# Value projection of a diffusion attention: two blocks a batch in place of four, one for two groups of heads

## The reference, cut to what matters

```
h = layernorm(x) * ln1_w + ln1_b
qk = (h @ Wqk).reshape(b, n, 16, 16).transpose(0, 2, 1, 3)
v = (h @ Wv).reshape(b, n, 16, 16).transpose(0, 2, 1, 3)
logits = (2 * qk @ qk^T - |qk_n|^2 - |qk_m|^2) / 4 * tau
out = softmax(logits) @ v        # per head, 512 x 512
y = out @ Wo
```

## Time and profile before

| | |
|---|---|
| time, median of 3 | 4381.61 us |
| the profiled execution | 4382.84 us, its span 4381.0 us |
| PE busy, whole span | 3709.8 us (85%) |
| DVE, ACT, POOL busy | 2415.1, 1752.6, 1619.3 us |
| the stage of the change | about 2767 to 3790 us of the span, with its head start and its end |
| granted TensorE clock over the span | 0.924 |
| value blocks (L2276) | 32 blocks, 512 PE instructions |

### The profile page before, as it was taken

One profiled execution on the slowest core, in us unless ns is written; L12 is line 12 of the kernel. 1 busy time (PEld: TensorE's weight loads), 2 busy tenths in 40 slices (PEclk: granted clock), 3 DMA queues, 4 the chain that ended last, 5 costly groups with the idle time before them and its releaser, 6 DMA issues. The chain is left out here.

```text
span 4381.0 us, 64166 instructions
## 1 busy us (share of the span) xinstructions
PE 3709.8 (85%) x17520; PEld 2209.8 (50%) x17584; DVE 2415.1 (55%) x6529; ACT 1752.6 (40%) x4010; POOL 1619.3 (37%) x1750
## 2 busy tenths in 40 slices
PE   6999999999689998997999899679999998459940
PEld 3555555566345555554555555335555554346630
DVE  6766676677465662224656433245566665345556
ACT  2544444455345554112555511035555545114420
POOL 2333333333466762004667512401222221352244
PEclk8999999999799999999999999879999999669975
DMA  6555665557201112443011211132222221249952
GB/s 103 71 74 68 84 84 79 71 65 92 67 25 39 48 43 99 158 164 105 34 38 48 74 46 60 41 79 53 61 56 54 54 50 47 89 166 312 312 169 70
DMA packets 230366, 378.28 MB, mean 86 GB/s; under 512 B 39822, under 2 KB 166099, under 8 KB 223699
## 3 DMA queue, kind: packets, MB, share of 16 engines
q1 hardware_dynamic: 216658, 355.13, 34.4%
q0 software_dynamic: 6144, 16.79, 1.2%
q10 hardware_dynamic: 7296, 3.22, 0.3%
HBM read 170.03 MB, written 84.93 MB: 58 GB/s over the span
## 5 line engine op out<-in xcount | busy, mean ns | idle before, releaser
L758 DVE CUSTOM_DVE_ANT_0 a_ps<-a_ps,a_mask 128x128 f32<-128x128 f32 (+3 forms) x1024 | 481.0, 513 | 219.1 <-PE a_ps L513 199.6
L2618 DVE TENSOR_REDUCE c_neg_max<-c_ps 128x1 f32<-128x512 f32 x512 | 340.8, 684 | 244.5 <-PE c_ps L2286 243.1
L2479 ACT ACTIVATE c_probsT<-c_ps 128x512 f32<-128x512 f32 x512 | 299.2, 598 | 400.1 <-PE c_ps L2298 391.2
L368 POOL TENSOR_SCALAR_AFFINE_SELECT a_probs_c<-a_probs_c 128x256 f32<-128x256 f32 (+1 forms) x384 | 185.8, 500 | 699.5 <-ACT a_probs_c L663 699.2
L663 ACT ACTIVATE a_probs_c<-a_ps 128x512 f32<-128x512 f32 x640 | 344.6, 603 | 119.5 <-PE a_ps L531 84.4
L513 PE MATMUL a_ps<-a_packed_qk 65*128 65x128 f32 (+3 forms) x1024 | 336.9, 373 | 53.5 <-DVE a_maxima L758 28.0
L1094 POOL TENSOR_TENSOR w_probs<-w_probs,w_inv 128x1024 f32<-128x1024 f32 x128 | 242.3, 1893 | 334.8 <-DVE w_inv L1457 334.8
L549 PE MATMUL a_ps<-a_probs_c,a_v 128*64 128x512 f32 (+3 forms) x2048 | 329.9, 468 | 1.8 <-POOL a_probs_c L368 0.8
L531 PE MATMUL a_ps<-a_packed_qk 67*128 67x512 f32 (+3 forms) x1024 | 288.8, 345 | 0.8 <-DMA a_packed_qk<-a_max_half 0.8
L2286 PE MATMUL c_ps<-c_packed_qk 68*128 68x512 f32 x512 | 263.2, 519 | 4.4 <-DVE c_neg_max L2618 2.2
L1349 ACT ACTIVATE w_probs<-w_ps_s,w_neg_max 128x256 f32<-128x256 f32 x512 | 236.0, 478 | 68.2 <-DVE w_neg_max L1452 66.9
(11 more groups left out here) (323 smaller groups left out, 7805.9 us busy)
## 6 DMA issues: line engine op xcount, KB each, us to landing
a_packed_qk<-a_halves SPq DMA_DIRECT2D x512, 128.0 KB, 4.6
d_w<-in_L_ffn_second SPq DMA_DIRECT2D x71, 516.0 KB, 5.0
d_w<-in_L_ffn_first SPq DMA_DIRECT2D x71, 512.0 KB, 5.1
rows_dram<-f_zeros SPq DMA_DIRECT2D x8, 4096.0 KB, 16.1
c_packed_qk<-c_halves SPq DMA_DIRECT2D x256, 128.0 KB, 2.4
w_v<-w_v_next SPq DMA_DIRECT2D x16, 1024.0 KB, 4.7
d_rows<-rows_dram SPq DMA_DIRECT2D x71, 128.0 KB, 4.3
mixed_dram<-d_y SPq DMA_DIRECT2D x71, 128.0 KB, 4.9
```

The source lines that it names most:

```text
L758: last = nc.vector.tensor_tensor_reduce(tile, tile, mask[:, (NT - 1 - i) * P:], 1.0, -3e38, ALU.add, ALU.max, accum_out=maxima_of[:, hd // ...
L2479: nc.scalar.activation(probsT[:, q % 2, r, :], ps_again[u % 2][:, :], ACT.Exp).then_inc(exp_done.sem, 1)
L2618: nc.vector.tensor_reduce(neg_max[:, g % 2, 0, s % GS:s % GS + 1], bank("s", s)[:, :], AX.X, ALU.max, negate=True).then_inc(max_ready.sem, 1)
```

## The change

The value projection makes one block for two groups: `project_v(b, f)` streams 128 columns of `wv` for each of the same eight weights, and fills the whole bank. There are two blocks a batch. Block 0 (groups 0 and 1) is made in step 60 of the batch before, where block 1 stood, and block 1 (groups 2 and 3) in step 26, where block 3 stood. The entries of steps 11 and 52 go. ACT copies 512 columns at a time in place of 256. `weigh` waits for block g // 2, the copy for the values' readers of two groups.

Since two uses leave the ring, the banks of all later uses shift, and the ring is filled up by two free places. `combine` on DVE gets one more wait, for its own operation of the group before.

```diff
-    EXTRA = {... 9: [("t", 2, -1)], 11: [("v", 2, 0)], ... 26: [("v", 3, 0)],
+    EXTRA = {... 9: [("t", 2, -1)],                    ... 26: [("v", 1, 0)],
-             52: [("v", 0, 1)], 53: [("z", 0, -1)], ... 60: [("v", 1, 1)]}
+             53: [("z", 0, -1)], ...                    60: [("v", 0, 1)]}
...
-            def project_v(b, j):
-                if j == 0:
+            def project_v(b, f):
+                if f == 0:
                     pe.wait_ge(rest_in.sem, 16 * len(rest))
-                cols = slice(HG * DH * j, HG * DH * (j + 1))
                 for t in range(NT):
                     for k in range(KD):
-                        last = nc.tensor.matmul(bank("v", j)[:, t * HG * DH:(t + 1) * HG * DH],
-                                                hT[:, k, t * P:(t + 1) * P], wv[:, k, cols], start=k == 0, stop=k == KD - 1)
+                        last = nc.tensor.matmul(bank("v", f)[:, t * P:(t + 1) * P], hT[:, k, t * P:(t + 1) * P],
+                                                wv[:, k, f * P:(f + 1) * P], start=k == 0, stop=k == KD - 1)
...
-                    pe.wait_ge(v_ready.sem, v_ready.at(b, g + 1))
+                    pe.wait_ge(v_ready.sem, v_ready.at(b, g // 2 + 1))
...
-            def evacuate_v(b, j, prior):
-                act.wait_ge(v_psum.sem, v_psum.at(b, j + 1))
+            def evacuate_v(b, f, prior):
+                act.wait_ge(v_psum.sem, v_psum.at(b, f + 1))
                 if prior:
-                    act.wait_ge(pv_done.sem, pv_done.at(ref(b, -1), NT * (j + 1)))
-                nc.scalar.copy(v[:, :, HG * j:HG * (j + 1), 0:DH],
-                               bank("v", j)[:, 0:NT * HG * DH].rearrange("p (t h d) -> p t h d", t=NT, d=DH))\
-                  .then_inc(v_ready.sem, 1)
+                    act.wait_ge(pv_done.sem, pv_done.at(ref(b, -1), NT * 2 * (f + 1)))
+                heads = 2 * HG
+                nc.scalar.copy(v[:, :, heads * f:heads * (f + 1), 0:DH],
+                               bank("v", f)[:, :].rearrange("p (t h d) -> p t h d", t=NT, d=DH)).then_inc(v_ready.sem, 1)
...
             def combine(b, g):
                 dve.wait_ge(sums_psum.sem, sums_psum.at(b, g + 1))
+                if g:
+                    dve.wait_ge(o_ready.sem, o_ready.at(b, g))
```

More of the change, by code:

```diff
@@ L1822, in diffusion_attention @@
     CC = float(N) ** -0.5
-    EXTRA = {0: [("m", 3, -1)], 2: [("q", 2, 0)], 6: [("q", 3, 0)], 9: [("t", 2, -1)], 11: [("v", 2, 0)],
[1 row of a table removed]
+    EXTRA = {0: [("m", 3, -1)], 2: [("q", 2, 0)], 6: [("q", 3, 0)], 9: [("t", 2, -1)],
[1 row of a table added]
              27: [("o", 1, -1)], 28: [("h", 0, 1)], 29: [("y", 0, -1)], 30: [("y", 1, -1)], 31: [("h", 1, 1)],
@@ L2020, in run @@
         max_packed = [signal(f"max_packed{j}", 16) for j in range(G)]
-        v_psum, v_ready = signal("v_psum", G), signal("v_ready", G)
+        v_psum, v_ready = signal("v_psum", G // 2), signal("v_ready", G // 2)
         scores_ready, max_ready = signal("scores_ready", STEPS), signal("max_ready", STEPS)
```

## The result

The changed kernel takes 4353.9 us (median of five runs, 4338.81 to 4362.72), beside 4381.61 us of the kernel before (4377.87 to 4393.85). The two medians lie 27.7 us apart. The ratio taken over all runs is 0.9926, with a 95% interval from 0.9903 to 0.9949: it is faster by 0.74%, or 32 us, where 21.3 us had been forecast. The profiled execution took 4347.98 us with a span of 4346.1.

What follows compares the result with a forecast made beforehand. PE bounds the kernel; gains of 15.5 (step 11), 6.4 (step 52) and 0.2 (prologue) less 0.8 us (wider blocks) make 21.3 us. From 4382.84 that gives 4361.5, and 4360 us for the median; range 4351 to 4371.

Steps and rivals of the forecast that it cites:

- What bounds: In the pipelined loop PE sets the pace, busy 97.46 us of a 106 us batch; DVE and ACT wait for it.
- The price of a block: A value block of 128 columns costs the old 1.71 to 1.81 us, since the weight load covers the doubled stream.
- The 0.05 us more: Loss for each widened block in steps 26 and 60, for its last, wider matmul: 16 x 0.05 = 0.8 us.
- Rival (c): The stream decides: a block of 128 columns takes twice 1.71 us, 5.3 us slower in all, 4387 us; chance 0.03.
- Step 11: Its block goes without a new wait: seven batches gain 1.81 us each, batch 0 gains 2.8; sum 15.5 us.
- rival (a): In step 11 a wait takes the place of the removed block, leaving a gain of 5.8 us: 4376 us; chance 0.07.
- Step 52: Its block goes, but z waits 0.74 us: batches 1 to 6 gain 0.81 us each, batch 0 1.5; sum 6.4.
- rival (b): The wait for x is shorter and all removed work is gained, 30.6 us: 4351 us; chance 0.05.
- Prologue: One of two value blocks before the first score goes; that score also needs the norms' DMAs, so gain 0.2 us.
- Batch 0: First batch, partly at the lower clock: gain of 2.8 us at step 11 and 1.5 us at step 52.
- Batches 1 to 6: Each gains 1.81 us at step 11 and 0.81 us at step 52, less 0.05 us for each widened block.
- rival (d): Lower-clock stretches of 13 us follow the new wait in step 53 of six batches, costing 39 us: 4399 us; chance 0.05.

Runs made afterwards that it cites:

- e_step11: The kernel before with only the value block of step 11 removed (groups 2 and 3 share step 26): 4366.78 us, ratio 0.9966.
- e_cover: The changed kernel with the norms of group 0 moved from step 50 to step 52, between x and z: 4345.80 us, ratio to before 0.9916.
- e_step52: The kernel before with only the value block of step 52 removed (groups 0 and 1 share step 60): 4377.87 us, ratio 0.9986.
- the second pair of profiles: Profiles of the kernel before and the changed kernel, both run again without edits: 4386.05 us (ratio 1.0002) and 4352.84 us (ratio 0.9925).
- r_after: The changed kernel run again without an edit: 4352.84 us, ratio to before 0.9925.
- the padded ones: The changed kernel with value block 1 repeating 8, 16 or 32 PE instructions a batch: 4365.86, 4378.61 and 4381.63 us.
- e_q3: The changed kernel with the queries block of step 6 put behind step 7 and the norms of step 12 behind step 13: 4365.09 us, ratio to before 0.9954.
- e_turn: `e_cover` with both turns of the normed input (steps 37, 38) put behind step 38: 4345.86 us, ratio to before 0.9923.
- e_pad8: The changed kernel with value block 1 repeating 32 PE instructions a batch, onto the same columns: 4381.63 us, ratio to before 1.0002.

## Why the prediction was right, and where it was not

**What bounds.** Right. PE sets the pace, and DVE and ACT gave up 32.0 and 27.3 us of waiting.

**The price of a block.** Right: the shape in the trace of before decided it. PE in order of time, block 0 of a batch and the score behind it:

```profile
3061.95 1.95 PE L2275 MATMUL c_ps<-c_wv,c_hT 128*128 128x128 f32 x16
3063.66 0.48 PE L2285 MATMUL c_ps<-c_packed_qk 68*128 68x512 f32 x1
```

It takes 3063.66 - 3061.95 = 1.71 us with 128 columns, as with 64. That the weight load covers the doubled stream, as the prediction said, fits this; no run takes the load apart from the stream. The 0.05 us more that the sum had for each can't be seen. Rival (c), twice that, is refuted.

**Step 11, batches 1 to 6.** Right in its order. PE there:

```profile
3082.11 1.06 PE L2312 MATMUL c_ps<-c_probsT,c_v 128*32 128x512 f32 x8
3083.10 0.50 PE L2285 MATMUL c_ps<-c_packed_qk 68*128 68x512 f32 x1
3083.44 0.39 PE L2297 MATMUL c_ps<-c_packed_qk 70*128 70x512 f32 x1
3083.76 1.89 PE L2266 MATMUL c_ps<-c_qsq,c_neg_norm 128*16 128x512 f32 x4
```

The norms start 3083.76 - 3082.11 = 1.65 us after the weighing, without a wait; before, with the block between them, it was 3099.27 - 3095.83 = 3.44 us. That is 1.79 us for the forecast 1.81, and rival (a) is refuted. `e_step11` measured the whole term at 13.7 us of weighted span for 15.5; some of that term lies in batch 0 at the lower level, where the weighted span counts half.

**Step 52.** Right to the last digit in a batch of the middle:

```profile
3048.53 1.13 PE L2372 MATMUL c_ps<-c_woc,c_cattn 128*128 128x256 f32 x4
...
3051.33 1.97 PE L2382 MATMUL c_ps<-c_mix,c_vcT 128*128 128x256 f32 x8 [0.74 <-DVE c_neg_max L2617]
3052.95 0.58 PE L2285 MATMUL c_ps<-c_packed_qk 68*128 68x512 f32 x1
```

From x to the score of step 54 it takes 3052.95 - 3048.53 = 4.42 us, and z waits 0.74 us, both as in the last batch before. The profile names DVE's maximum as releaser; ACT's row says which wait it is:

```profile
3050.65 0.58 ACT L2520 COPY c_mix<-c_ps 128x512 f32<-128x512 f32 x1
```

The copy of x ends at 3051.23, and z starts 0.1 us later. In all six batches x to that score takes 4.41 to 4.42 us, a gain of 0.81 and not 1.71, so rival (b) is refuted as a mechanism, though the time came out near its 4351 us. `e_cover` took that wait away. `e_step52` measured the term at 7.7 us of weighted span for 6.4.

**Prologue.** 0.2 forecast, 0.33 came. PE's norms of the prologue in the kernel before:

```profile
2875.47 3.45 PE L2266 MATMUL c_ps<-c_qsq,c_neg_norm 128*16 128x512 f32 x4 [3.36 <-DVE c_halves L2593]
```

The changed kernel there, with the norms of step 12 and of step 50 in batch 0:

```profile
2875.94 3.46 PE L2266 MATMUL c_ps<-c_qsq,c_neg_norm 128*16 128x512 f32 x4 [3.36 <-DVE c_halves L2592]
...
2884.01 0.93 PE L2285 MATMUL c_ps<-c_packed_qk 68*128 68x512 f32 x3 [2.55 <-DMA c_packed_qk<-c_norms]
...
2897.17 3.28 PE L2266 MATMUL c_ps<-c_qsq,c_neg_norm 128*16 128x512 f32 x4 [0.82 <-DVE c_halves L2592]
...
2948.56 1.89 PE L2266 MATMUL c_ps<-c_qsq,c_neg_norm 128*16 128x512 f32 x4
```

From the norms to the first score it takes 2884.01 - 2875.94 = 8.07 us, where it took 2883.86 - 2875.47 = 8.39; in the second pair of profiles it is 8.06 and 8.40. The score now waits for the DMA of the norms. The removed block mostly uncovered that wait.

**Batch 0: a term too small.** Forecast 2.8 + 1.5 = 4.3 us, measured 8.0. In parts: from the first score to the norms of step 12 it takes 13.16 us where it took 16.54, a gain of 3.4 for 2.8, with the forecast wait for the split (0.82 us). From there to the norms of step 50 it takes 51.39 us, where before, to this row,

```profile
2955.39 1.89 PE L2266 MATMUL c_ps<-c_qsq,c_neg_norm 128*16 128x512 f32 x4
```

it took 54.99. That is a gain of 3.6 us in 38 steps in which nothing was removed, and the sum had nothing for it. The rest gained 1.1 for 1.5. What differs in those 38 steps is the clock. The long stretch at the lower level ended near 2917 us and not near 2930; over all batch 0 it is about 24 us and not 41. In the second pair of profiles it is 31 and 41, and the batch gained 8.1 us again. Batch 0 of `r_after`, `e_step11` and `e_step52`, columns as in the section on the result:

```profile
2889.65:2972.38 82.73, 71.29 (x267) 34.24 (x267) 52.31 (x94) 36.76 (x66) 8.61 (x12) 0.81 0.35 85
...
2878.22:2962.06 83.84, 72.80 (x283) 35.88 (x283) 52.38 (x94) 36.87 (x68) 8.23 (x12) 0.82 0.35 84
...
2879.17:2969.59 90.42, 79.40 (x282) 39.56 (x282) 52.36 (x94) 37.06 (x67) 8.51 (x12) 0.77 0.32 78
```

This excess comes with the block of step 11. Without that block alone (`e_step11`) batch 0 is 6.7 us shorter, where the sum had 2.8 for it, and the long stretch ends some 33 us behind the first score, as in the changed kernel. With it (`e_step52`) the batch is as long as before, 90.42 us. The two kernels without a change show 90.50 and 90.84. Every other kernel without the block, the padded ones too, has 81.6 to 86.4 us. Not all time at the lower level costs the same, though: the two profiles of the changed kernel differ by about 7 us of it early in the batch, and by 0.3 us in length.

**Batches 1 to 6: a term too small.** Forecast 1.81 + 0.81 - 0.10 = 2.5 us each and measured 3.7: 105.6 to 101.9 us, the means of six batches in two profiles of each kernel. In weighted time the gain is 101.9 to 99.5, thus 2.4, the forecast value. The other 1.2 to 1.3 us are clock: 7.4 us a batch at the lower level before, 4.9 after. Over six batches that is 7 us beyond the sum. Here neither part alone did it: a batch of `e_step11` and of `e_step52` has 7.7 and 7.0 us in its profile.

**The step that failed** is the last one of the sum: "The profiled execution took 4382.84 us, 1.84 of it outside the span; less 21.3 that is 4361.5." It took the clock of that execution over as it was, in batch 0 too, where the rows had shown a stretch of 13 us at the lower level with PE busy for 11.76. The removed blocks brought what was worked out, 22.3 us of weighted span for 21.3. On top came 18 us less at the lower level, worth 9 us. The prediction spoke of the clock only as something that could be lost, in rival (d), and gave it "a few us"; the range let it move the time only to the slower side. In neither profile of the changed kernel does a stretch at the lower level begin within 6 us behind the new wait of z in batches 1 to 6, so (d) is refuted, and the mean granted clock rose from 0.9236 to 0.9251. That the median of 4353.9 us still lies between 4351 and 4371 is luck: the room on that side was made for (b), which didn't come. The ratio puts the changed kernel at 4381.61 x 0.9926 = 4349 us, below it.

**What stays open:** what decides whether such a stretch comes, and so why it came less often in batches 1 to 6. Most of them in the loop begin behind PE's waits for the split (1.6 us), for POOL's norm (1.8) or for the doubled maxima (1.3), but not behind each of these, and `e_q3` shows them behind three waits of under 0.7 us. Taking waits away (`e_q3`, `e_turn`) did not lower the time at that level, and adding work did not raise it steadily.

## What to carry to other kernels

A small matmul here costs the same with 64 and with 128 columns, so two that stream different columns past the same weights are worth making into one; read the price from a shape in the trace that already has the new width. Look for the place where the new order already stands, as in a last batch without a follower: it gave the new wait to 0.01 us. Where the granted clock lies between its levels, forecast span times clock, and put a range, to both sides, on the time at the lower level by itself: here it lay between 643 and 687 us, without following the work or the waits.

## What the runs showed of the hardware

- f32 matmuls with 128 x 128 weights: 107 ns an instruction in a row, with 64 and with 128 columns alike (1.71 us for x16), and 3.42 us more for 32 more in `e_pad8`.
- Span times granted clock has a standard deviation of 4.3 us between executions of one kernel (76 of the kernel before, 4034 to 4055 us); that of their times is 6.1 us (4369 to 4397).
- With the value block in step 11, batch 0 took 90.4 to 90.8 us in three profiles and stood 41 us of them at the lower level. Without it, it took 82.5 to 83.8 us in the two profiles of the changed kernel and in `e_step11`, with 23 to 31 us at the lower level.
- The same 28 us of weighted span, given back in `e_pad8`, cost all the gain in time, but with 655 us at the lower level for 669. `e_q3` has 35 us less weighted span than `e_pad8` and 32 us more at the lower level.
